# Projection to q, k and v: three fp16 passes over split operands in place of fp32

## What is computed

```
xn = layernorm(x)
q = xn @ wq.T      # 512 columns
k = xn @ wk.T      # 128 columns
v = xn @ wv.T      # 128 columns
q = q * cos + rotate_half(q) * sin
k = k * cos + rotate_half(k) * sin
```

## Time and profile before

| | us |
|---|---|
| median of 3 runs | 1540.02 |
| the three runs | 1542.85, 1540.02, 1538.23 |
| profiled execution, first to last instruction (span) | 1535.8 |
| profiled execution, its own time | not recorded apart from its span; the median lies 4.2 above the span |
| TensorE busy in the span | 1354.5 (88%) |
| VectorE busy | 1031.6 (67%) |
| ScalarE busy | 835.2 (54%) |
| GpSimd busy | 464.0 (30%) |
| mean granted TensorE clock, as a share of 2.4 GHz | 0.942 |
| stage `project`, from the first transpose to the start of attention's loads | 525.7 to 641.1 |

### The profile page before, as it was taken

The page is one execution under the profiler, slowest core; times in us unless marked ns, Lnnn a source line. Parts: engine busy times, 40 slices in busy tenths (PEclk is TensorE's granted clock), DMA queues, the critical chain, the costliest instruction groups (busy, mean ns, idle before and its releaser), DMA issues. The chain is left out here.

```text
span 1535.8 us, 35207 instructions
## 1 busy us (share of the span) xinstructions
PE 1354.5 (88%) x10502; PEld 719.6 (47%) x10598; DVE 1031.6 (67%) x3495; ACT 835.2 (54%) x1550; POOL 464.0 (30%) x1396
## 2 busy tenths in 40 slices
PE   8948999999999699389989899898989989986996
PEld 4413444444444355245545455455545545543563
DVE  5884545545453289588878788787878878861553
ACT  2613423314031167367768677676767768773553
POOL 3650000000000233233433343333433433331664
PEclk9976999999999899779999999999999999998997
DMA  9300000000000045701000111001111000002221
GB/s 338 131 12 30 1 1 0 0 0 0 0 0 0 4 128 159 223 28 38 17 28 35 39 38 38 11 34 35 38 39 38 26 18 35 13 8 49 62 70 48
DMA packets 65106, 69.52 MB, mean 45 GB/s; under 512 B 35214, under 2 KB 53774, under 8 KB 64300
## 3 DMA queue, kind: packets, MB, share of 16 engines
q1 hardware_dynamic: 64940, 67.38, 13.4%
HBM read 36.96 MB, written 19.92 MB: 37 GB/s over the span
## 5 line engine op out<-in xcount | busy, mean ns | idle before, releaser
L1321 DVE TENSOR_REDUCE arena<-bank 128x32 f32<-128x512 f32 (+3 forms) x768 | 395.6, 550 | 111.0 <-PE bank L1168 55.7
L1259 ACT ACTIVATE arena<-bank 128x512 f32<-128x512 f32 x576 | 337.0, 613 | 177.6 <-PE bank L1179 103.4
L1165 PE MATMUL bank<-arena 96*128 96x512 bf16 (+3 forms) x768 | 249.4, 349 | 27.0 <-issue 19.3
L1179 PE MATMUL bank<-arena 123*128 123x512 bf16 x576 | 225.5, 397 | 10.2 <-ACT arena L1259 7.1
L1198 PE MATMUL bank<-arena 128*32 128x128 f32 x4608 | 171.0, 276 | 12.6 <-ACT arena L1259 12.4
L577 PE MATMUL bank<-arena 128*128 128x512 f16 (+1 forms) x704 | 168.0, 381 | 0.0
L1417 POOL TENSOR_SCALAR arena<-arena 128x128 bf16<-128x128 bf16 x384 | 142.6, 371 | 46.9 <-DVE arena L1367 22.9
L586 PE MATMUL bank<-arena 128*128 128x512 f32 (+1 forms) x352 | 152.7, 593 | 1.6 <-DVE arena L710 1.6
L649 ACT ACTIVATE arena<-bank 128x512 f32<-128x512 f32 (+1 forms) x88 | 52.5, 596 | 173.8 <-PE bank L574 173.7
L1405 POOL TENSOR_TENSOR arena<-arena 128x4 f32<-128x4 f32 x128 | 25.4, 199 | 378.1 <-DVEq L1339 378.0
L1198 PEld LDWEIGHTS bank<-arena 128*32 128x32 f32 x4608 | 119.4, 109 | 43.0 <-ACT arena L1259 24.6
(11 more groups left out here) (186 smaller groups left out, 2207.9 us busy)
## 6 DMA issues: line engine op xcount, KB each, us to landing
arena<-qk_rows SPq DMA_DIRECT2D x16, 960.0 KB, 5.0
qk_rows<-arena SPq DMA_DIRECT2D x16, 768.0 KB, 4.1
arena<-arena SPq DMA_DIRECT2D x32, 256.0 KB, 2.9
arena<-in_x SPq DMA_DIRECT2D x4, 1024.0 KB, 12.3
out<-arena SPq DMA_DIRECT2D x16, 256.0 KB, 2.2
qk_rows<-arena SPq DMA_DIRECT2D x16, 192.0 KB, 4.6
arena<-in_down_qT SPq DMA_DIRECT2D x1, 2816.0 KB, 25.8
arena<-in_up_qT SPq DMA_DIRECT2D x1, 2752.0 KB, 18.0
```

The costliest lines, as they stand in the source:

```text
L1165: last = pe.matmul(bank[:, 0:k1 - k0], query_aug[st.slot][0:ROWS, h * P:(h + 1) * P], key_aug[st.p][0:ROWS, k0:k1], start=True, stop=not d ...
L1179: last = pe.matmul(bank[:, :], key_aug[st.p][0:KROWS, j * P:(j + 1) * P], query_aug[st.slot][0:KROWS, f * N:(f + 1) * N], start=True, stop ...
L1259: act.activation(probs[u % PROBS], back_bank[u % 2][:, :], ACT.Exp, scale=float(HD) ** -0.5).then_inc(probs_ready, 1)
L1321: dve.tensor_reduce(out=cm[:, h * 64 + k0 // CHUNK:h * 64 + k1 // CHUNK], in_=score_bank[bank_of_score(front, number)][:, 0:k1 - k0].rearr ...
```

## The change

The weights are multiplied by 64 and split into an fp16 part and an fp16 rest, once, by three GpSimd instructions over 128 x 3072 elements in the `gated` stage, after the weights' load and ahead of GpSimd's loop. In `project` ScalarE's `keep` writes the turned tile as fp16 (`x_high`) rather than fp32. VectorE gets a new instruction per tile, `keep_rest`, which subtracts `x_high` from the turned tile in PSUM and writes the fp16 rest. `feed` is 12 fp16 matmuls of 512 columns and 12 of 256 columns: high times high, high times the weights' rest, and x's rest times high. TensorE waits for `x_rest` ahead of the ninth. The evacuations scale by 1/64. VectorE's loop is peeled by one turn, so that the last turn has no `keep_rest`.

```diff
@@ -501,6 +501,15 @@
                     branch_add(dve, m, dve_seq, p, y[(u * 2 + p) % Y], u * 2 + p).then_inc(added, 1)
 
 
+W_UNIT = 64.0
+
+
+def qkv_weights(m):
+
+    n = DC * QKV
+    return m.f32(WQKV_AT, n), m.f16(WQKV_AT + n, n), m.f16(WQKV_AT + n + n // 2, n)
+
+
 def gated(nc, m, s, dram):
 
 
@@ -745,6 +754,15 @@
                 for t in range(G):
                     pool.wait_ge(stats_ready, g * G + (t + 1))
                     branch_rstd(pool, m, pool_seq, t % 2).then_inc(branch_rstd_ready, 1)
+            w, w_high, w_rest = qkv_weights(m)
+            pool.wait_ge(m.qkv_in, 16)
+            pool_seq.mark(pool.tensor_scalar(out=w, in0=w, scalar1=W_UNIT, scalar2=None, op0=ALU.mult))
+            pool_seq.wait(pool)
+            pool_seq.mark(pool.tensor_copy(w_high, w))
+            pool_seq.wait(pool)
+            pool_seq.mark(pool.tensor_tensor(out=w_rest, in0=w, in1=w_high, op=ALU.subtract))
+            pool_seq.wait(pool)
+            pool_seq.settle()
             over_groups(pool, group)
 
 
@@ -753,16 +771,18 @@
 
 
 
-    W = m.f32(WQKV_AT, DC * QKV)
+    _, w_high, w_rest = qkv_weights(m)
     take = m.taker(WORK, ARENA - SEQ)
-    xn, xT = [take(D) for _ in range(2)], [take(D) for _ in range(2)]
+    xn = [take(D) for _ in range(2)]
+    x_high, x_rest = [take(D, F16) for _ in range(2)], [take(D, F16) for _ in range(2)]
     raw, spun = [take(QK) for _ in range(2)], [take(QK) for _ in range(2)]
     rotated = [take(QK) for _ in range(2)]
     part = [[take(QK, BF16) for _ in range(PARTS)] for _ in range(2)]
     q_rows, k_rows = [take(HEADS * ROWS, BF16) for _ in range(2)], [take(KV * ROWS, BF16) for _ in range(2)]
     key_rows = take(SEQ)
     v_all = m.f32(V_AT, GROUPS * SEQ_TILES * 32)
-    rstd_ready, xn_ready, turned, xT_ready = s("c_rstd"), s("c_xn"), s("c_turned"), s("c_xT")
+    rstd_ready, xn_ready, turned = s("c_rstd"), s("c_xn"), s("c_turned")
+    x_high_ready, x_rest_ready = s("c_x_high"), s("c_x_rest")
     products, raw_ready, v_ready, spun_ready = s("c_products"), s("c_raw"), s("c_v"), s("c_spun")
     rotated_ready, high_ready, high_rows_ready = s("c_rotated"), s("c_high"), s("c_high_rows")
     rows_ready, rows_out = s("c_rows_ready"), [s(f"c_rows_out{b}") for b in range(2)]
@@ -805,17 +825,17 @@
                 last.then_inc(turned, 1)
 
             def feed(k, b):
-                pe.wait_ge(xT_ready, k + 1)
+                pe.wait_ge(x_high_ready, k + 1)
                 pe.wait_ge(v_ready, k + 1)
-                for dc in range(DC):
-                    pe.matmul(m.banks[2 + b][:, :], xT[b][:, dc * P:(dc + 1) * P], W[:, dc * QKV:dc * QKV + D],
-                              start=dc == 0, stop=dc == DC - 1)
-                for dc in range(DC):
-                    last = pe.matmul(m.banks[4 + b][:, 0:QKV - D], xT[b][:, dc * P:(dc + 1) * P], W[:, dc * QKV + D:(dc + 1) * QKV],
-                                     start=dc == 0, stop=dc == DC - 1)
+                terms = [(x, w, dc) for x, w in ((x_high[b], w_high), (x_high[b], w_rest), (x_rest[b], w_high)) for dc in range(DC)]
+                for bank, first, end in ((m.banks[2 + b], 0, D), (m.banks[4 + b], D, QKV)):
+                    for n, (x, w, dc) in enumerate(terms):
+                        if n == 2 * DC and first == 0:
+                            pe.wait_ge(x_rest_ready, k + 1)
+                        last = pe.matmul(bank[:, 0:end - first], x[:, dc * P:(dc + 1) * P], w[:, dc * QKV + first:dc * QKV + end],
+                                         start=n == 0, stop=n == len(terms) - 1)
                 last.then_inc(products, 1)
 
-            pe.wait_ge(m.qkv_in, 16)
             for b in range(2):
                 turn(b, b)
             with pe.Fori(0, SEQ_TILES - 1) as i:
@@ -834,16 +854,17 @@
 
             def keep(k, b):
                 act.wait_ge(turned, k + 1)
-                act.activation(xT[b], m.banks[b][:, :], ACT.Copy).then_inc(xT_ready, 1)
+                act.activation(x_high[b], m.banks[b][:, :], ACT.Copy).then_inc(x_high_ready, 1)
 
             def evacuate(i, b):
                 k = i * 2 + b
                 act.wait_ge(products, k + 1)
                 act.wait_ge(rotated_ready, k + 1)
-                act.activation(raw[b][:, 0:D], m.banks[2 + b][:, :], ACT.Copy)
-                act.activation(raw[b][:, D:QK], m.banks[4 + b][:, 0:QK - D], ACT.Copy).then_inc(raw_ready, 1)
+                act.activation(raw[b][:, 0:D], m.banks[2 + b][:, :], ACT.Copy, scale=1.0 / W_UNIT)
+                act.activation(raw[b][:, D:QK], m.banks[4 + b][:, 0:QK - D], ACT.Copy, scale=1.0 / W_UNIT).then_inc(raw_ready, 1)
                 v = v_all.rearrange("p (b k t c) -> p b k t c", b=BATCH, k=KV, t=SEQ_TILES)[:, b]
-                act.activation(v[:, :, ds(i, 1), 0:HD].squeeze(2), heads(m.banks[4 + b][:, QK - D:QKV - D]), ACT.Copy).then_inc(v_ready, 1)
+                act.activation(v[:, :, ds(i, 1), 0:HD].squeeze(2), heads(m.banks[4 + b][:, QK - D:QKV - D]), ACT.Copy,
+                               scale=1.0 / W_UNIT).then_inc(v_ready, 1)
 
             def cut(i, b):
                 k = i * 2 + b
@@ -899,11 +920,11 @@
 
         @block.vector
         def _(dve):
-            dve.wait_ge(rows_in, 16)
-            for k in range(2):
-                dve.tensor_copy(m.key_aug[k][ROWS:KROWS, :], key_rows[ROWS:KROWS, :])
-            with dve.Fori(0, SEQ_TILES) as i:
-                dve_seq.enter(i, 12)
+            def keep_rest(k, b):
+                dve.wait_ge(x_high_ready, k + 1)
+                dve.tensor_tensor(out=x_rest[b], in0=m.banks[b][:, :], in1=x_high[b], op=ALU.subtract).then_inc(x_rest_ready, 1)
+
+            def rotate_and_cut(i, last):
                 cos = m.cos.rearrange("p (t d) -> p t d", d=HD)[:, ds(i, 1), :]
                 for b in range(2):
                     k = i * 2 + b
@@ -913,6 +934,9 @@
                     dve_seq.wait(dve)
                     dve.wait_ge(spun_ready, k + 1)
                     dve.tensor_tensor(out=rotated[b], in0=rotated[b], in1=spun[b], op=ALU.add).then_inc(rotated_ready, 1)
+                if not last:
+                    for b in range(2):
+                        keep_rest(i * 2 + (2 + b), b)
                 for b in range(2):
                     k = i * 2 + b
                     high, mid, low = part[b]
@@ -931,7 +955,17 @@
                     dve_seq.wait(dve)
                     dve.tensor_copy(kk[:, :, 2:3, :], k_of(low, 1))
                     dve.tensor_copy(q[:, :, 5:6, :], q_of(low, 1)).then_inc(rows_ready, 1)
-            dve_seq.leave(SEQ_TILES)
+
+            for b in range(2):
+                keep_rest(b, b)
+            dve.wait_ge(rows_in, 16)
+            for k in range(2):
+                dve.tensor_copy(m.key_aug[k][ROWS:KROWS, :], key_rows[ROWS:KROWS, :])
+            with dve.Fori(0, SEQ_TILES - 1) as i:
+                dve_seq.enter(i, 12)
+                rotate_and_cut(i, False)
+            dve_seq.leave(SEQ_TILES - 1)
+            rotate_and_cut(SEQ_TILES - 1, True)
 
 
 def attention(nc, m, s, dram):
```

## The result

The changed kernel takes 1546.43 us (median of 6 runs, 1544.24 to 1547.23) against 1539.86 for the kernel before beside it. The ratio is 1.0041, with a 95% interval of 1.0029 to 1.0053: 6.6 us slower, where 5.3 were forecast.

What follows compares the result with a forecast made beforehand. TensorE's loop of 12.10 us was taken as the bound, VectorE close behind. First turn 0.0, six turns +6.8 and last turn -1.5 summed to +5.3 on 1540.0, giving 1545.3 us, range 1535 to 1554.

Steps and rivals of the forecast that it cites:

- VectorE becomes the bound: Loop of project: VectorE's turn 13.31 us against 9.54 on TensorE, whose saved 2.56 us turn into waiting.
- Four collisions of 0.66: Loop of project: each of GpSimd's four instructions per turn delays a VectorE instruction by 0.66 us, 2.64 in all.
- Rivals A: GpSimd's instructions find gaps and VectorE hides the rest: six turns at 10.8 us, 1529 in all, faster; chance 0.11.
- B: About no change: three collisions or a cheaper keep_rest, period 12.5 to 12.7 us, 1541 in all; chance 0.22.
- D: Dearer collisions: each costs a whole GpSimd record, 1.07 us, turn 14.9, 1557 in all; chance 0.05.
- keep_rest at 0.61, outside the lock: VectorE in project: each costs 0.61 us, two per turn 1.22, and, reading PSUM, should not collide with GpSimd.
- First turn: Start of project: first feed ends 1.3 us sooner, second turn starts at 551.4 against 551.35, so 0.0.
- Six turns at +1.14: Loop of project: six turns at 13.31 us in place of 12.17 cost +6.8 us.
- Last turn: End of project: no keep_rest; the 0.82 wait for GpSimd and one collision of 0.66 go, -1.5 us.
- The weights: GpSimd's preparation in gated: 12.9 us, ending at 131.9, cost 0; a dearer multiply covered by a 3.65 us wait.
- Rival C, the clock: TensorE's clock halves after its 3 to 4 us pause in feed; 1550 us expected, 1565 if all slow; chance 0.12.
- the slack of 2.8: Loop of project: the 10.5 us loop through TensorE's wait for x_rest stays under VectorE's 13.31, 2.8 us to spare.

Runs made afterwards that it cites:

- no_rest: Changed kernel without keep_rest, the third fp16 pass taking x_high again, TensorE's matmul count unchanged; 1539.35 us, 0.9988 of the kernel before.
- spin_on_vector: Changed kernel with GpSimd's four multiplies per turn moved to VectorE; 1540.29 us, 0.9998 of the kernel before.
- two_passes: Changed kernel without the pass of x_high with the weights' rest, 8 matmuls less per feed; 1542.06 us, 1.0016 of the kernel before.
- rest_between: Changed kernel with both keep_rest moved ahead of the second tile's rotation in VectorE's turn; 1543.34 us, 1.0028 of the kernel before.
- evac_first: Changed kernel, GpSimd's multiplies on VectorE, second part's cast on ScalarE, VectorE's cutting reordered, first tile's evacuation ahead of normalizations; 1531.11 us, 0.9950 of the kernel before.
- before_spin: Kernel before the change with GpSimd's multiplies moved to VectorE; 1538.25 us, 0.9991 of the kernel before.

## Why the prediction was right, point by point

- **VectorE becomes the bound: right.** Its turn was 13.35 us against 13.31. "No idle time" held in four of the six turns; in the other two it waited 0.82 for GpSimd. `no_rest` and `spin_on_vector` moved the period as its work says, and `two_passes`, which relieves TensorE, did not move it. `rest_between` shows the same period at full clock.
- **Four collisions of 0.66: right.** Four stretched instructions per turn stand in the timeline, by 0.66 to 0.69 each. In other turns a pair of them cost 0.54 each (L946, 1.03 for 0.49; L948, 1.36 for 0.83). `no_rest` shows the turn with none of them, and `spin_on_vector` what their going is worth. Rivals A and B needed fewer or cheaper ones and fall; D needed 1.07 each and falls too.
- **keep_rest at 0.61, outside the lock: right.** Two took 1.20 us, each record 0.68. The prediction states the rule of the Trainium skill (page "SBUF — State Buffer", section "Who interferes with whom") too widely, though: the page excepts two-port modes, which it says copies and casts can enter, from what it says of a single SBUF input. Here the copies L951 and L952, with one SBUF input, were stretched all the same. Free by the rows are `keep_rest` and L731, both with one operand in PSUM.
- **First turn: close.** The first rotation started 1.42 us sooner (forecast 1.3), the second turn 0.37 sooner (forecast 0.0).
- **Six turns at +1.14: a little too much.** They cost 78.91 - 72.99 = +5.9 us, where +6.8 was forecast, since the second turn took 12.01, the next four 13.2 to 13.3 and the seventh 13.84. The second had two stretched instructions and not four: 9.45 + 1.20 + 1.36 = 12.01.
- **Last turn: half right.** It gave -0.8 and not -1.5. The wait went, but a collision stayed, since GpSimd still worked on the last pair when VectorE arrived:

```profile
630.40 2.03 POOL L917 TENSOR_TENSOR arena<-arena 128x320 f32<-128x320 f32 x2 [1.03 <-issue]
...
631.65 1.47 DVE L932 TENSOR_TENSOR arena<-arena 128x640 f32<-128x640 f32 x1
```

- **Sum.** -0.37 + 5.92 - 0.80 = +4.75 in `project`, forecast +5.3. The three terms missed by -0.4, -0.9 and +0.7 us, so part of the agreement is errors that cancel. The measured +6.6 holds about 2 us more, which arise in `attention` in both profiles and are not explained; the prediction had put everything outside `project` at 0. That the whole was missed by only 1.3 is luck in part, since `project` was forecast 0.55 too dear.
- **The weights: the term was mis-sized, the verdict right.** The multiply took 7.97 us, not the 3.05 of a cast, and more than the 6.8 that I had given as its upper end. GpSimd was done at 136.5, not 131.9. The cover named for this case, the wait ahead of L688 (now L697), did its work.
- **Rival C, the clock: there, and cheap.** The clock fell as C said (0.86 to 0.93 in the windows of 12 us from 552 on), although TensorE's pause was only 2.01 us and not 3 to 4. The two belong together: the half clock took 1.67 us per turn, and 2.01 + 1.67 is about the pause that was forecast for full clock. That stayed inside the slack of 2.8. `rest_between` had the clock at full over three turns and they were no shorter, so the rival's price here was nothing.

## What to carry to other kernels

Before you relieve a busy engine, read how much idle time the next one has in the same loop, and count what the relief asks of it. Here 0.8 us of idle time on VectorE was to pay for 1.2 us of new work and for a fourth collision of 0.66, and 2.6 us saved on TensorE bought nothing. And count a helper engine's help at its net value: GpSimd's four multiplies saved VectorE 1.6 us and cost it 2.6 in collisions, which showed only as a few VectorE records of 1.5 us between records of 0.8. With that new bound lightened, in `evac_first`, the whole was 0.5% faster than the kernel before. How much of it needs the fp16 form was not measured: no run has the same relief of VectorE with fp32 matmuls. That `before_spin` stood at TensorE's 12.10 per turn, where `evac_first` took 11.27, speaks for a part.

## What the runs showed of the hardware that was not expected

A multiply by a constant on GpSimd, 128 x 3072 fp32 in place, took 7.97 us, and the subtraction of two operands of the same size 6.01 and the cast 2.74. The multiply, with one tensor operand, was the dearest.

A VectorE cast with both ends in SBUF was held until the GpSimd instruction it had met was over: L688, started at 133.90 inside L763, ended at 136.82, 0.29 us after it. In free time it takes 0.42.

The clock fell to half behind a pause of 2.01 us in the middle of the feed (granted 0.86 over the window). In `evac_first`, with a pause of 1.83 us, it stayed at full. But the length of the pause does not decide it. In `rest_between` pauses of 3.05 and 3.08 us were followed by full clock, and in `spin_on_vector` a pause of the same 2.60 us was followed by half clock in some turns and by full clock in others. In `two_passes` a third of the multiplying had been taken away, and the clock fell to 0.77: part of what TensorE was spared came back as slower cycles. A stage with TensorE off the path pays this from its slack. The Trainium skill, page "TensorE: Matmul & The Clock Gate", section "What's actually happening", says that activity releases the throttle. `two_passes`, with the least matmul work and the lowest clock, agrees in direction; why the clock falls in one turn and not in another these runs do not explain.
